# Causal attention with ALiBi: row maxima from three leading products, two heads side by side in the two halves of the array, one maximum over two banks, and the scaling on GpSimd

## The reference

```python
q = (x @ q_w + q_b).reshape(Bx, Tx, NH, HD).transpose(0, 2, 1, 3)
kv = (x @ kv_w + kv_b).reshape(Bx, Tx, 2, NH, HD).transpose(2, 0, 3, 1, 4)
k, v = (kv[0], kv[1])
att = jnp.einsum('bhqd,bhkd->bhqk', q, k) * (1.0 / np.sqrt(HD))
att = att + build_alibi_bias(NH, Tx)[None]
att = jnp.where(causal[None, None], att, -jnp.inf)
att = jax.nn.softmax(att, axis=-1)
y = jnp.einsum('bhqk,bhkd->bhqd', att, v)
y = y.transpose(0, 2, 1, 3).reshape(Bx, Tx, Cx)
return y @ o_w + o_b
```

## Time and profile before

| | |
|---|---|
| three runs, us | 2729.39, 2735.36, 2735.55 (median 2735.36) |
| profiled execution, its own time, us | 2729.97 |
| its span, us | 2727.9 |
| mean granted clock of TensorE | 0.978 |
| PE, DVE, ACT, POOL busy | 95%, 85%, 76%, 50% of the span |
| matmuls, and instructions of DVE | 21670, 4175 |

### The profile page before, as it was taken

One profiled execution on the slowest core, in us unless ns is written; L12 is line 12 of the kernel. 1 busy time (PEld: TensorE's weight loads), 2 busy tenths in 40 slices (PEclk: granted clock), 3 DMA queues, 4 the chain that ended last, 5 costly groups with the idle time before them and its releaser, 6 DMA issues.

```text
span 2727.9 us, 57513 instructions
## 1 busy us (share of the span) xinstructions
PE 2598.3 (95%) x21670; PEld 1637.9 (60%) x21670; DVE 2321.1 (85%) x4175; ACT 2059.8 (76%) x3887; POOL 1373.4 (50%) x1768
## 2 busy tenths in 40 slices
PE   6779999999997999999999999999999999999998
PEld 4569989999996444545445454454544545455454
DVE  3468888888886998999989998899998999999993
ACT  2248878877884687888887887788887887887886
POOL 2235555555653365464654645546464464654644
PEclk9889999999998899999999999999999999999999
DMA  2015575545555646556474564655546556474540
GB/s 73 1 44 171 179 189 186 173 164 177 176 178 165 106 74 123 80 99 106 73 127 75 104 105 68 122 82 98 100 79 122 82 97 102 77 127 77 103 89 17
DMA packets 315172, 299.58 MB, mean 110 GB/s; under 512 B 97174, under 2 KB 265516, under 8 KB 314668
## 3 DMA queue, kind: packets, MB, share of 16 engines
...
...
## 4 chain that ended last, share of the span: by engine, by line
PE 54%; ACT 6%; DMA 5%; issue 1%; SPq 0%; DVE 0%; POOL 0%; POOLq 0%; ACTq 0%
PE t_y L1570 19%; PE t_r L1554 16%; PE t_a L1505 12%; ACT t_prob L1599 6%; DMA scr_m<-t_mrows 4%; PE t_a L1538 4%; PE t_r L1516 3%; DMA t_q<-scr_m 1%; DMA t_k<-t_blockb 0%; DVE t_mxc L1647 0%; ACT t_mrows L1616 0%; SPq L1411 0%; ACT t_near L1608 0%; SPq L1417 0%; POOL t_prob L1744 0%
## 5 line engine op out<-in xcount | busy, mean ns | idle before, releaser
L1599 ACT ACTIVATE t_prob<-t_r 128x512 f32<-128x512 f32 (+1 forms) x2432 | 1261.4, 599 | 289.5 <-PE t_r L1554 285.4
L1647 DVE TENSOR_REDUCE t_mxc<-t_a 128x1 f32<-128x512 f32 (+3 forms) x1920 | 1129.3, 643 | 105.4 <-PE t_a L1505 102.7
L1554 PE MATMUL t_r<-t_q,t_k 109*128 109x128 bf16 (+4 forms) x4608 | 831.7, 275 | 31.1 <-DMA t_q<-scr_m 20.9
L1505 PE MATMUL t_a<-t_k,t_q 99*128 99x512 bf16 (+3 forms) x2560 | 650.1, 320 | 1.5 <-DVE t_mxc L1647 1.0
L1750 POOL TENSOR_SCALAR_AFFINE_SELECT t_near<-t_near 128x512 f32<-128x512 f32 x512 | 332.7, 650 | 532.3 <-ACT t_near L1608 532.1
L1570 PE MATMUL t_y<-t_prob,t_v 128*32 128x512 f32 (+3 forms) x6144 | 588.0, 496 | 0.0
L1554 PEld LDWEIGHTS t_r<-t_q,t_k 102*128 102x128 bf16 (+1 forms) x4608 | 373.6, 98 | 342.9 <-ACT t_prob L1599 133.1
L1744 POOL TENSOR_SCALAR_AFFINE_SELECT t_prob<-t_prob 128x512 f32<-128x512 f32 x512 | 322.5, 637 | 276.9 <-ACT t_prob L1599 276.9
L1608 ACT COPY t_near<-t_r 128x512 f32<-128x512 f32 x512 | 307.5, 602 | 82.6 <-PE t_r L1516 65.6
L1505 PEld LDWEIGHTS t_a<-t_k,t_q 99*128 99x128 bf16 x2560 | 210.8, 98 | 228.5 <-DVE t_mxc L1647 155.0
L1570 PEld LDWEIGHTS t_y<-t_prob,t_v 128*32 128x32 f32 x6144 | 157.7, 109 | 257.3 <-issue 182.4
...
## 6 DMA issues: line engine op xcount, KB each, us to landing
t_q<-scr_q SPq DMA_DIRECT2D x384, 128.0 KB, 4.0
t_k<-scr_k SPq DMA_DIRECT2D x384, 128.0 KB, 6.6
...
```

What stands on the lines that cost most here:

```text
L1505: mm = pe.matmul(abank[n % A_BANKS][:, x * w:(x + 1) * w], q_op[t % NG][0:KA, h0 + x, i * P:(i + 1) * P], k_op[t % NG][0:KA, h0 + x, k0:k0 ...
L1554: mm = pe.matmul(ring[n % RING_BANKS][:, s * w + lo:s * w + hi], k_op[g][0:deep, h0 + s, j * P:(j + 1) * P], q_op[g][0:deep, h0 + s, q0 + ...
L1599: nc.scalar.activation(prob[:, q % SLOTS, h0:h0 + m, 0:w], ring[n % RING_BANKS][:, 0:m * w].rearrange("p (h n) -> p h n", h=m), ACT.Exp).t ...
L1647: V.tensor_reduce(mxc[:, t % 2, k0 // 512, h0:h0 + m, i], abank[n % A_BANKS][:, 0:m * w].rearrange("p (h n) -> p h n", h=m), AX.X, ALU.max ...
```

## The change

**Operands.** The three leading products (high with high, high with middle, middle with high) and the three bias rows now lie together, 51 rows (NMAIN): for the first two heads of a group from row 0, for the other two from row 64 (`MAIN`). The three smaller products stand in the rows left over (`OTHER`), and 16 rows of zeros fill a gap in the second pair. So KA, KB and KM are one value for each pair of heads: 99 and 115, 102 and 118, 109 and 125. Each load is of two heads instead of four: 24 DMAs for q and k and one for v, in five pieces (`load_operands`), and 12 DMAs of constants (`load_constants`).

**Maxima.** Off the diagonal only the 51 leading rows are multiplied. The maximum is only a shift that cancels in the softmax. Two heads, one of each pair, go one after the other into the two halves of the rows, each into its own bank of a slot of two banks. One DVE reduction takes 1024 or 768 columns. There are 15 units a group, A_SLOTS = 2 slots of two banks, and the ring has 3 banks instead of 4. All maxima lie in one tensor, and the join is one reduction.

**The rest.** The scaling goes from DVE to GpSimd. The maximum comes back in two DMAs. `plan()` knows the new costs (a pair of matmuls is charged once, and no charge for a change of the array's division around a maximum), puts logits or maxima first when ScalarE or DVE is short of work, no longer keeps weigh pieces together, issues loads by time in five pieces, and loads the residual after the batch before is stored. `first_load(2)` comes after the first lift. The diff, cut to its core:

```diff
 NPOS = 3
-NSLOT = 6
-KA = NPOS + NSLOT * HD
-KB = KA + 3
-KM = KB + P // 16 - 1
-Q_PART = [0, 0, 0, 1, 1, 2]
-K_PART = [0, 1, 2, 0, 1, 0]
+SUB = 16
+NMASK = P // SUB - 1
+NMAIN = NPOS + 3 * HD
+MAIN, OTHER = (0, 64), (NMAIN, 0)
+KA = (NMAIN + 3 * HD, 64 + NMAIN)
+KB = tuple(k + 3 for k in KA)
+KM = tuple(k + NMASK for k in KB)
 PRODUCTS = ("w0", "wq", "wk", "wv", "wr", "wkk", "wvv")
...
+def load_constants(eng, a, q, k, blockb, zeros, g, done):
+    each = lambda t, n: t.rearrange("p (o n) -> p o n", o=1).to_broadcast([n, GH * QT // 2, P])
+    for e in range(2):
+        rows = lambda t, lo, n: t[lo:lo + n, 2 * e:2 * e + 2, :]
+        tiled = lambda t, lo, n: rows(t, lo, n).rearrange("p h (i n) -> p (h i) n", n=P)
+        at = g * GH + 2 * e
+        eng.dma_start(rows(q, MAIN[e], NPOS), a["q_pos"][:, at:at + 2, :]).then_inc(done, 16)
+        eng.dma_start(rows(k, MAIN[e], NPOS), a["k_pos"][:, 0:2, :]).then_inc(done, 16)
+        eng.dma_start(rows(k, KA[e], 3), a["k_one"][:, 0:2, :]).then_inc(done, 16)
+        eng.dma_start(tiled(q, KB[e], NMASK), each(a["bmask"][SUB:P:SUB, :], NMASK)).then_inc(done, 16)
+        eng.dma_start(tiled(k, KB[e], NMASK), each(blockb[:, :], NMASK)).then_inc(done, 16)
+        if e == 1:
+            eng.dma_start(tiled(q, 3 * HD, 64 - 3 * HD), each(zeros[:, :], 64 - 3 * HD)).then_inc(done, 16)
+            eng.dma_start(tiled(k, 3 * HD, 64 - 3 * HD), each(zeros[:, :], 64 - 3 * HD)).then_inc(done, 16)
...
+def load_operands(eng, scr, q, k, v, b, g, done, piece):
+    qs, ks = (scr[n].rearrange("s b (h d) t -> s b d h t", d=HD) for n in ("qs", "ks"))
+    if piece < LOAD_PIECES - 1:
+        e, (op, src, parts) = piece // 2, ((q, qs, Q_PARTS), (k, ks, K_PARTS))[piece % 2]
+        at = g * GH + 2 * e
+        for lo, which in ((MAIN[e] + NPOS, parts[0]), (OTHER[e], parts[1])):
+            for n, s in enumerate(which):
+                eng.dma_start(op[lo + n * HD:lo + (n + 1) * HD, 2 * e:2 * e + 2, :],
+                              src[s, b][:, at:at + 2, :]).then_inc(done, 16)
+    else:
+        vs = scr["v"].rearrange("b (j p) (g c) -> b g p j c", p=P, g=NG)
+        eng.dma_start(v[:, :, 0:GH * VW], vs[b, g]).then_inc(done, 16)
...
-    out = []
-    for i in range(1, QT):
-        for k0 in range(0, i * P, 512):
-            w = min(512, i * P - k0)
-            out += [(i, k0, w, h, per_bank(w)) for h in range(0, GH, per_bank(w))]
-    return out
+    units = [(i, 512, (h, h + 2)) for i in range(QT // 2, QT) for h in range(2)]
+    units += [(i, 384, (h, h + 2)) for i in (3, 7) for h in range(2)]
+    units += [(i, 256, (0, 2, 1, 3)) for i in (2, 6)]
+    units += [(1, 128, (0, 2, 1, 3))]
...
-A_BANKS, RING_BANKS, SLOTS = 3, 4, 6
+A_SLOTS, RING_BANKS, SLOTS = 2, 3, 6
 OUTS = 4
...
-        if t % NG == 1 and c == 0:
-            pl.order["SP"] += [("residual", t // NG, 0)]
-            for x in range(OUTS):
-                for z in range(2):
-                    pl.give("POOL", end + 8000 + 3000 * (2 * x + z), t + 1.2 + 0.25 * x, ("shift", t // NG, 2 * x + z), 1300)
+        if t == 1 and c == 0:
+            residual(0, end)
+    def residual(b, end):
+        pl.issue.append((end, "residual", b, 0))
+        for n in range(2 * OUTS):
+            pl.give("POOL", end + 8000 + 3000 * n, NG * b + 2.2 + 0.12 * n, ("shift", b, n), 1300)
...
-        stay = [e for e in able if tiled and e[1] == "weigh" and e[0] < min(able)[0] + 0.1]
-        rank, kind, t, x = min(stay or able)
+        behind = lambda n: max(0.0, pl.free[n] - now) + sum(e[3] for e in pl.todo[n])
+        dry = [k for n, bound, kinds in (("ACT", 1000, ("exp", "diag")), ("DVE", 600, ("max",))) if behind(n) < bound
+               for k in kinds]
+        rank, kind, t, x = min([e for e in able if e[1] in dry] or able)
         streams["max" if kind == "rows" else kind].pop()
         pl.order["PE"].append((kind, t, x))
         if (kind == "weigh") != tiled:
             tiled, now = not tiled, now + 90
         if kind == "max":
-            i, k0, w, h, n = MAX_UNITS[x]
-            now += n * mm(w)
+            i, w, h = MAX_UNITS[x]
+            n = len(h) * (2 if w == P else 1)
+            now += n // 2 * max(mm(w), 112) + 10
             slot_freed.append(("max", t, x))
...
             if x == NQ - 1 and t + NG < GROUPS:
-                pl.order["SP"].append(("load", t, 0))
+                pl.issue += [(now + 3000 * z, "load", t, z) for z in range(LOAD_PIECES)]
...
-            last = lambda end, t=t: pl.order["SP"].append(("store", t, 0))
+            def last(end, t=t):
+                pl.issue.append((end, "store", t, 0))
+                if t + 1 < B:
+                    residual(t + 1, end + 6000)
             pl.give("DVE", now + 165, rank, ("sum", t, x), 616, last if x == OUTS - 1 else None, "slot")
     pl.settle(pl.FAR)
+    pl.order["SP"] = [e[1:] for e in sorted(pl.issue)]
...
-                                 scr["m"][g].rearrange("(s n) q -> s (n q)", s=3)).then_inc(s_m[g], 16)
+                    m_rows = scr["m"][g].rearrange("(s e n) q -> s e (n q)", s=3, e=2)
+                    for e in range(2):
+                        sp.dma_start(q_op[g][KA[e]:KB[e], 2 * e:2 * e + 2, :].rearrange("p h t -> p (h t)"),
+                                     m_rows[:, e, :]).then_inc(s_m[g], 16)
+                    if t == 0:
+                        first_load(2)
...
-                i, k0, w, h0, m = MAX_UNITS[u]
+                i, w, heads = MAX_UNITS[u]
                 if u == 0:
                     operands_in(t)
                 free_slot(n)
-                for x in range(m):
-                    mm = pe.matmul(abank[n % A_BANKS][:, x * w:(x + 1) * w],
-                                   q_op[t % NG][0:KA, h0 + x, i * P:(i + 1) * P],
-                                   k_op[t % NG][0:KA, h0 + x, k0:k0 + w], start=True, stop=True)
+                blocks = [(i, 0), (i + 4, 512)] if w == P else [(i % 4 if w < 512 else i, 0)] if i < 4 or w == 512 else [(i, 512)]
+                at = 0
+                for pair in range(len(heads) // 2):
+                    for i, k0 in blocks:
+                        for e in range(2):
+                            h = heads[2 * pair + e]
+                            mm = pe.matmul(abank[n % A_SLOTS][:, 512 * e + at:512 * e + at + w],
+                                           q_op[t % NG][MAIN[e]:MAIN[e] + NMAIN, h, i * P:(i + 1) * P],
+                                           k_op[t % NG][MAIN[e]:MAIN[e] + NMAIN, h, k0:k0 + w], start=True, stop=True)
+                        at += w
...
+                to = QT + i if i > 3 and w < 512 else i
+                if w == P:
+                    out, pieces = mine[:, :, i:i + QT + 5:QT + 4], dict(h=GH, s=2, n=P)
+                    data = abank[n % A_SLOTS][:, :].rearrange("p (h s n) -> p h s n", **pieces)
+                elif w == 2 * P:
+                    out = mine[:, :, to]
+                    data = abank[n % A_SLOTS][:, :].rearrange("p (h n) -> p h n", h=GH)
+                else:
+                    out = mine[:, heads[0]:GH:2, to]
+                    data = abank[n % A_SLOTS][:, :].rearrange("p (e n) -> p e n", e=2)[:, :, 0:w]
+                V.tensor_reduce(out, data, AX.X, ALU.max, negate=True).then_inc(s_au, 1)
...
-                V.tensor_tensor(flat(mxj[:, :, :]), flat(mxd[:, z, :, :]), flat(mxc[:, z, 0, :, :]), ALU.min).then_inc(s_join, 1)
-                dve.wait_ge(s_join, 2 * t + 1)
-                V.tensor_tensor(flat(mx[:, z, :, :]), flat(mxj[:, :, :]), flat(mxc[:, z, 1, :, :]), ALU.min).then_inc(s_join, 1)
+                V.tensor_reduce(mx[:, z, :, :], mxc[:, z, :, :].rearrange("p h (c i) -> p h i c", i=QT),
+                                AX.X, ALU.min).then_inc(s_join, 1)
...
+            def scale(t, c):
+                pool.wait_ge(s_y, y_step["invert", t, c])
+                if t % 2 == 0 and t > 1:
+                    pool.wait_ge(s_y, y_step["back", t - 1, c])
+                pool.tensor_tensor(yn[:, c, :, t % 2, :], ysw[:, c, :, 0:HD],
+                                   rec[:, c, :].rearrange("p (b o) -> p b o", o=1).to_broadcast([P, QT * 2, HD]),
+                                   ALU.mult).then_inc(s_ys, 1)
```

170 lines of the change are left out of this document (64 added, 106 removed).

## The result

The changed kernel takes 2751.28 us (median of 5 runs, 2749.57 to 2755.26), the kernel before 2735.36 beside it: **0.76% slower, ratio 1.0076 [1.0052, 1.0100]**. The forecast was 2724 and slightly faster, with a range of 2645 to 2790. So the time lies in the range and the direction is wrong. The ratio is that of the means, 2751.6 and 2731.0: the kernel before ran five times, and its fifth run, 3206.66 us in a slower state of the chip, is left out. The profiled execution spans 2753.5 us, before 2727.9.

What follows compares the result with a forecast made beforehand. The prediction took PE to bound the kernel, DVE close behind: steady part -32 us, start and projections +24, sum -8 from the profiled 2730.0, that is 2722, taken as 2724 us; range 2645 to 2790.

Steps and rivals of the forecast that it cites:

- Maxima on PE: Off-diagonal maxima: paired half-row matmuls run at once, 14336 columns become 7168; -2.6 us a group after 0.45 for exposed costs.
- Changes of division: PE's order: 31.3 more switches of the array's division a group at 0.095 us each, +3.0 us a group.
- Rival (a): Maxima on PE: halves need no change of division, only the product with v's extra changes cost; 2617 us, chance 12%.
- Waits of PE: Steady attention: new load order removes 0.6 us, logits-first order and filled gaps 0.3; -0.9 us a group.
- DVE and GpSimd: Steady attention: DVE falls from 26.0 to 23.9 us a group, GpSimd takes 1.3 more; no effect on time.
- Steady sum: Attention's steady part: -2.6 + 3.0 - 0.9 = -0.5 us a group, x 63 = -32 us.
- Start, +20, and projections, +4: SP's queue: more DMAs delay lift 1 and group 2's operands, +20 us; a late store in the projections, +4 us.
- those of pairs: Sign in PE's sequence: 512-column pairs start within 0.02 us, next 0.22 later; 0.31 from full matmul to pair and back.
- of scr_m: Sign in PE's waits: waiting for scr_m comes to under 0.2 us a group.
- lifts 27.8 us apart: Sign in the steady attention: lifts follow each other 27.8 us apart on average; over 28.4 would say rival (c).
- rival (c): Paired matmuls on PE: weight loads lie bare, +0.5 to +1.0 us a group; 2756 to 2787 us, chance 18%.
- being wrong as to cause: Sign in PE's waits: the forecast's cause would be wrong if DVE or ACT ended most waits.

Runs made afterwards that it cites:

- e2: Changed kernel, same order, but maxima are products of all rows on the full array, no halves: 2805.11 us, ratio 1.0266 to the kernel before.
- e7: e4 plus the changed kernel's rule for PE's order (logits first when ScalarE runs dry, pieces not kept together), ring of 4 banks: 2770.30 us, ratio 1.0152.
- e4: Kernel before with only the changed kernel's order of SP (residual load by planner's time, operand loads in five pieces): 2706.28 us, ratio 0.9900.
- e8: e7 with a ring of 3 banks instead of 4 and the matching planner condition for first diagonal blocks: 2778.47 us, ratio 1.0184 to the kernel before.
- e11: Changed kernel with SP's idle gap at the start filled by loads, and the scaling planned and run on VectorE again: 2720.27 us, ratio 0.9951.
- e13: e11 with its orders of PE, ACT and SP kept, but the scaling executed on GpSimd: 2723.19 us, ratio 0.9981 to the kernel before.
- e12: Changed kernel with SP's start gap filled by loads, scaling planned on GpSimd but executed on VectorE, other orders kept: 2743.25 us, ratio 1.0062.
- e1: Changed kernel with group 3's first load and the 17 loads of output weights moved behind lift 1: 2765.47 us, ratio 1.0119 to the kernel before.

## Why the prediction was wrong

By its own steps, a group in the steady part, forecast and what the runs showed:

- *Maxima on PE, -2.6*: -3.1 (e2). The mechanism was right, the size too small by 0.3 to 0.5. The 0.01 a pair is 3 to 4 ns, and no second weight load of 128-column pairs lies bare. The estimate by the Trainium skill (TensorE: Matmul & The Clock Gate, part 3), with 4 ns for a further member, was -2.97. The trace agrees for halves, and has 6 to 7 ns for each further quarter of the product with v.
- *Changes of division, +3.0*: 31.4 more changes at 0.095, **+3.0**. Right in count and size, and the earlier trace rows told it beforehand; 2.0 of it is the maxima's (e2), 0.9 the product with v's (e7). Rival (a) is out, and the rule of the Trainium skill (TensorEngine Tiling, key properties) that changing the mode drains the engine agrees with it: each change costs time. That it is a drain no run shows.
- *Waits of PE, -0.9*: **0.0** (-0.2 if only what exceeds 25 ns counts). **This step failed.** The first part, 0.6 for the transfers, came out at 0.48 (e4), but it was taken from 0.8 us a group that counted the same waits twice; counted once they are 21.9 us, 0.44 a group. The second was the thought that the new rule and PE's own longer work would take 0.3 more away and that the shorter ring was a cause on the other side of equal weight. In sum the rule took nothing (e7: 1.33 and 1.33), the bank cost 0.27 net (e8), and from there to the changed kernel 0.2 more came with the halves and with the order that goes with planning the scaling on GpSimd (1.60 to 1.79). That order alone makes 0.4 (e11, e13). So the 0.5 saved at the transfers was given back at the ring.
- *DVE and GpSimd, nothing*: right for the operations (e12, e13: up to 0.12), wrong for what their costs do to the order of PE (e11: 0.35 in the period). The forecast treated the order as given; it is a result of the costs.
- *Steady sum, -0.5*: measured +0.10. The terms above (-3.1 + 3.0 + 0.0) give -0.1. The other 0.2 is a term that the forecast left out. Where one piece of the product with v follows another directly, each of its two passes starts 23 ns sooner than the count allows (409 ns behind the last start of a 512-column pass, not 433). The stretch has 520 such starts before, 10.5 a group or 0.24 us, and 20 in the changed kernel, since the new rule takes the pieces one at a time. A piece split off so costs 0.05 us beside its two changes.
- *Start, +20, and projections, +4*: +21.5 and +3.0 by the fifth and the first lift. Right, and lift 1 at 950.84 where 947 was named. But the prediction took lift 1's lateness for the cause with group 2's wait inside it; e1 shows that the wait for operands is the larger part and that each later item of SP's list costs in its turn.

Had the term for the waits been 0, the sum would have been 2724 + 57 = 2781; the 0.5 of the maxima that was missed brings it back to 2750. These two errors offset each other in part, and that the time came within 27 us of the forecast owes something to luck. Of the signs named in the prediction, those of pairs, of the first lift within 2.4 us and of scr_m (0.1 us a group) came true; lifts 27.8 us apart (28.47) did not. By its period it would be rival (c), but (c)'s mechanism, bare weight loads, is not there. What it said of being wrong as to cause held: ScalarE ends most waits.
